# Three products of a feature group added in the same 128 PSUM columns, in place of two halves summed by VectorE

## The reference

```python
x = x + ffn0(cond0(x, itok, weights))        # the stage of this case
x = x + moe1(lora1(x, W, A, Bm, scalings, itok2))
# cond0: out[b, d, t] = sum_c x[b, c, t] * weights[itok[b]][c, d]     (64 x 64 per batch entry)
# ffn0:  gate_w, up_w, down_w = Catmull-Rom interpolations of control points, dense [2048 x 512]
#        inter = silu(h @ gate_w.T) * (h @ up_w.T);  out = inter @ down_w.T
```

## Time and profile before

| | |
|---|---|
| median of 3 runs | 1525.37 us |
| lowest and highest run | 1524.51, 1527.99 us |
| span of the profiled execution | 1560.4 us |
| busy in it: PE, PEld, DVE, ACT, POOL | 1373.9, 1236.1, 744.1, 441.3, 735.8 us |
| mean granted TensorE clock | 0.943 |

### The profile page before, as it was taken

How to read it: one execution, slowest core, us unless ns; L and a number is a source line. 1 busy time by engine, 2 the same in 40 slices (tenths; PEclk the granted TensorE clock), 3 DMA queues, 4 the chain that set the end, 5 groups by cost and what they waited for, 6 DMA issues and landing times. The chain is left out here.

```text
span 1560.4 us, 28551 instructions
## 1 busy us (share of the span) xinstructions
PE 1373.9 (88%) x8494; PEld 1236.1 (79%) x8495; DVE 744.1 (48%) x1603; ACT 441.3 (28%) x1025; POOL 735.8 (47%) x1199
## 2 busy tenths in 40 slices
PE   2131699999999999999999999947999999999996
PEld 1111588888888888888888889947999999989995
DVE  3298555555555555555554344432333333333332
ACT  3133333333333333333322322202222222222221
POOL 6608444454444444444452134433555555555554
PEclk9755799999999999999999899978999999999998
DMA  4034153222333333333332844312476476474443
GB/s 147 3 112 155 59 155 112 104 105 99 118 127 127 127 127 126 126 122 118 127 100 113 309 137 155 114 44 54 81 188 189 90 186 177 86 194 79 75 76 66
DMA packets 89920, 187.48 MB, mean 120 GB/s; under 512 B 15111, under 2 KB 40079, under 8 KB 85665
## 3 DMA queue, kind: packets, MB, share of 16 engines
q1 hardware_dynamic: 61778, 134.02, 25.0%
q0 software_dynamic: 22016, 43.35, 14.1%
q10 hardware_dynamic: 6096, 9.73, 1.8%
HBM read 110.97 MB, written 76.19 MB: 120 GB/s over the span
## 5 line engine op out<-in xcount | busy, mean ns | idle before, releaser
L948 POOL TENSOR_TENSOR in_lo<-inner,in_hi 128x256 fp32r<-128x256 f32 x256 | 187.2, 731 | 293.0 <-DVE in_hi L1144 293.0
L1023 PE MATMUL bank<-down_hi,in_hi 128*128 128x512 f32 x512 | 203.1, 397 | 0.0
L1024 PE MATMUL bank<-down_lo,in_hi 128*128 128x512 f32 x512 | 203.0, 396 | 0.0
L1025 PE MATMUL bank<-down_hi,in_lo 128*128 128x512 f32 x512 | 202.1, 395 | 0.0
L1654 PE MATMUL bank<-slots,zt_hi 128*128 x568 | 190.6, 336 | 4.6 <-DVE zt_lo L1743 3.0
L1576 POOL TENSOR_TENSOR idle<-small 128x1 f32<-128x1 f32 x284 | 93.6, 333 | 196.6 <-DMA out<-result,scatter_at 116.3
L1656 PE MATMUL bank<-slots,zt_lo 128*128 x568 | 183.7, 323 | 0.0
L1655 PE MATMUL bank<-slots,zt_hi 128*128 x568 | 183.0, 322 | 0.0
L972 PE MATMUL bank<-f_hi,gu_hi 92*128 92x256 f32 x512 | 161.7, 316 | 1.3 <-POOL f_lo L940 1.3
L1153 DVE TENSOR_TENSOR inner<-silu_all,bank 128x256 f32<-128x256 f32 x256 | 106.4, 416 | 83.9 <-ACT silu_all L1086 81.7
L973 PE MATMUL bank<-f_lo,gu_hi 92*128 92x256 f32 x512 | 144.2, 282 | 0.0
(11 more groups left out here) (218 smaller groups left out, 3283.7 us busy)
## 6 DMA issues: line engine op xcount, KB each, us to landing
gate_up_dram<-split_gu SPq DMA_DIRECT2D x16, 1408.0 KB, 4.9
slots<-gate_up_dram SPq DMA_DIRECT2D x16, 1408.0 KB
x_both<-in_x SPq DMA_DIRECT2D x32, 512.0 KB
expert_down_dram<-split_down SPq DMA_DIRECT2D x16, 768.0 KB, 7.2
slots<-expert_down_dram SPq DMA_DIRECT2D x16, 768.0 KB
out<-x_both SPq DMA_DIRECT2D x16, 512.0 KB, 3.2
x<-out SPq DMA_DIRECT2D x8, 1024.0 KB, 5.8
raw_down<-in_down_proj SPq DMA_DIRECT2D x16, 352.0 KB, 7.4
```

The source lines that it names most:

```text
L948: nc.gpsimd.tensor_tensor(in_lo[:, c % RING, :], inner[c % INNER][:, :], in_hi[:, c % RING, :].bitcast(F32), ALU.subtract).then_inc(in_don ...
L1023: nc.tensor.matmul(psum[bank][:, :], in_hi[:, c % RING, rows], down_hi[:, c, :], start=(c == 0), stop=False)
L1024: nc.tensor.matmul(psum[bank][:, :], in_hi[:, c % RING, rows], down_lo[:, c, :], start=False, stop=False)
L1025: ins = nc.tensor.matmul(psum[bank][:, :], in_lo[:, c % RING, rows], down_hi[:, c, :], start=False, stop=(c == IC - 1))
```

## The change

The three products of a half all go to the same 128 columns of the bank, so that the bank holds the finished sum and a tile's group takes 256 columns rather than 512. ScalarE copies from the bank to `f_hi`, VectorE subtracts from the bank to `f_lo` and raises `drained`, and `chunk` waits for that. `f_sum`, `f_done` and GpSimd's `features` are gone.

```diff
-        f_sum = [sb(f"f_sum{b}", [NF, TILE]) for b in range(2)]
...
-                def features(t, g):
-
-                    pool.wait_ge(f_high, GROUPS * t + g + 1)
-                    nc.gpsimd.tensor_tensor(f_lo[:, g, :], f_sum[g % 2][:, :], f_hi[:, g, :].bitcast(F32), ALU.subtract).then_inc(f_done, 1)
...
                     for s in range(SUB):
-                        at, both = psum[bank][0:NF, s * 2 * P:(s + 1) * 2 * P], pair[:, s, :, :].rearrange("p l n -> p (l n)")
-                        nc.tensor.matmul(at, feat_hi[:, s, g, :], both, start=True, stop=False)
-                        ins = nc.tensor.matmul(at[:, 0:P], feat_lo[:, s, g, :], pair_hi[:, s, :], start=False, stop=True)
+                        at = psum[bank][0:NF, s * P:(s + 1) * P]
+                        nc.tensor.matmul(at, feat_hi[:, s, g, :], pair_hi[:, s, :], start=True, stop=False)
+                        nc.tensor.matmul(at, feat_hi[:, s, g, :], pair_lo[:, s, :], start=False, stop=False)
+                        ins = nc.tensor.matmul(at, feat_lo[:, s, g, :], pair_hi[:, s, :], start=False, stop=True)
                     ins.then_inc(filled[bank], 1)
...
-                        pe.wait_ge(f_done, GROUPS * t + g + 1)
+                        pe.wait_ge(drained[feat_bank(t, g)], use_feat(t, g) + 2)
...
-                    act.wait_ge(drained[feat_bank(t, g)], use_feat(t, g) + 2)
-                    nc.scalar.activation(f_hi[:, g, :], f_sum[g % 2][:, :], ACT.Copy).then_inc(f_high, 1)
+                    bank = feat_bank(t, g)
+                    act.wait_ge(filled[bank], use_feat(t, g) + 1)
+                    nc.scalar.activation(f_hi[:, g, :], psum[bank][0:NF, 0:TILE], ACT.Copy).then_inc(f_high, 1)
...
-                    dve.wait_ge(filled[bank], use_feat(t, g) + 1)
-                    if not (first_tile(t) and g < 2):
-
-                        dve.wait_ge(f_done, GROUPS * t + g - 1)
-                    nc.vector.tensor_reduce(f_sum[g % 2][:, :].rearrange("p (s n) -> p s n", s=SUB),
-                                            view(psum[bank][0:NF, :], 0, [[2 * P, SUB], [1, P], [P, 2]]), AX.X, ALU.add).then_inc(drained[bank], 1)
+                    dve.wait_ge(f_high, GROUPS * t + g + 1)
+                    nc.vector.tensor_tensor(f_lo[:, g, :], psum[bank][0:NF, 0:TILE], f_hi[:, g, :].bitcast(F32),
+                                            ALU.subtract).then_inc(drained[bank], 1)
```

More of the change, by code:

```diff
@@ L763, in first_ffn @@
         cond_loaded, pair_high, pair_done = sem("cond_loaded"), sem("pair_high"), sem("pair_done")
-        mom_high, raw_high, f_high, f_done = (sem(n) for n in ("mom_high", "raw_high", "f_high", "f_done"))
+        mom_high, raw_high, f_high = (sem(n) for n in ("mom_high", "raw_high", "f_high"))
         raw_loaded, split_high = sem("raw_loaded"), sem("split_high")
@@ L935, in gather_cond, with body @@
                                                      bass.IndirectOffsetOnAxis(ap=cond_now[:, s:s + 1], axis=0)).then_inc(cond_loaded, 16)
-                def features(t, g):
-                    pool.wait_ge(f_high, GROUPS * t + g + 1)
-                    nc.gpsimd.tensor_tensor(f_lo[:, g, :], f_sum[g % 2][:, :], f_hi[:, g, :].bitcast(F32), ALU.subtract).then_inc(f_done, 1)
-                def body(t, gather, has_next):
+                def body(t, gather):
                     for c in range(IC):
-                        if first_tile(t) and c < FIRST_FEATS:
-                            features(t, GU_BANKS + c)
                         pool.wait_ge(in_high, IC * t + c + 1)
@@ L953, in body @@
                             gather_cond(t + 2)
-                        if has_next and c in FEAT_AT:
-                            features(t + 1, FEAT_AT[c])
                 gather_cond(0)
@@ L959, in _ @@
                 gather_cond(1)
-                for g in range(GU_BANKS):
-                    features(0, g)
-                body(0, True, True)
+                body(0, True)
                 with pool.Fori(1, NT - 1) as t:
-                    body(t, True, True)
-                body(NT - 1, False, False)
+                    body(t, True)
+                body(NT - 1, False)
                 pool.wait_ge(cond_loaded, 16 * SUB * (NT + 1))
```

## The result

| | before | changed |
|---|---|---|
| median, us | 1524.97 (4 runs, 1524.51 to 1527.99) | 1533.39 (4 runs, 1532.74 to 1535.08) |
| ratio | | 1.0055, 95% interval 1.0039 to 1.0071 |

The change makes the kernel slower by 8.4 us, 0.55%. The forecast was slower, 1530.2 within 1523.5 to 1535.5. In a second comparison the changed kernel stood at 1.0070 (1.0055 to 1.0085), 1536.59 against 1524.63.

A forecast was written before the change was run, and what follows sets the result against it. The prediction took TensorE to bound the feed-forward stage behind its first 37 us. Feature groups +11.3 us and the start -6.5 gave +4.8, carried over from the median 1525.37 to 1530.2 us, range 1523.5 to 1535.5.

The forecast's parts named there:

- Bound and cover: First feed-forward layer: TensorE bounds it behind the first 37 us and covers the other engines' work; no new wait, 0.
- A group on TensorE: Feature group: 316 ns becomes 5 x 82 = 410, 94 more; 120 groups outside tile 0 give +11.3 us.
- last slot: Slot of a feature group's last matmul: the load behind it belongs to the next line, before and after alike.
- The start: Tile 0: earlier f_lo brings the first down matmul 4.75 us earlier; with the clock staying full, -6.5 us together.
- with TensorE filled up to 175.1 ... I expect it to stay full: Tile 0: clock stays full, idle under half a microsecond at a time; 3.6 us of later half clock take 1.8.
- Rival 1: Tile 0: the clock falls again, start gives only -1.7 us; +9.6 us, 1535.0; chance 0.2.
- the rounds: Tile 0: three rounds of a group and a chunk, 2.14 us each before, estimated at 1.5 us after.
- The sum: Whole kernel: +11.3 - 6.5 = +4.8 us, carried over unscaled to 1530.2 us.
- Rivals 2 and 3: Feature groups: repeated feat_hi load free, 1524.7, chance 0.12; loads hide behind narrow matmuls, 1516.4, chance 0.06.
- Rival 4: Start gives back less, as unprofiled runs may lack the slump; between the forecast and 1536; chance 0.12.

The follow-up runs named there:

- wide kernel: Changed kernel with TensorE's feature matmuls of before (256 and 128 columns) and VectorE subtracting, then adding, in two steps; ratio to before 0.9991.
- before's second profile: The kernel before, unchanged, profiled once more beside the changed kernel; span 1524.5 us.
- the transposes ahead: Changed kernel plus twenty identity transposes into an idle bank in tile 0, before the wait for the condition pair; ratios to before 1.0068 and 1.0062.
- short loads: Changed kernel with 64 of 92 feature columns as weights in the feature matmuls, chunks keeping 92 rows; ratio to before 0.9965.

## Why the prediction was right, and where its sum was off

**Bound and cover: right.** TensorE is busy without a gap behind 200 us in the changed kernel too, and nothing waits for f_lo or the feature bank. The wide kernel shows that the other engines' part is worth nothing in steady state.

**A group on TensorE: right in kind, 9 ns low.** The slot was forecast at 82 ns and its starts are 0.08 apart; the runs with 64 and 128 columns of weights fix the cause. Per group the period gives 0.82/8 = 103 ns, not 94: +12.3 us, not +11.3. The surplus is in the last slot, which the prediction took to be the same before and after. That holds where a chunk follows (0.17 to L973 in the earlier trace rows, 0.17 to L960 after): averaged over the groups between 200 and 800 us, such a group, counted up to the second matmul behind it, costs 87 ns more than before. Where transposes follow, as behind three groups in four, it costs 108 to 113 more: read without rounding, the first two transposes are 0.11 apart in the kernel before and 0.13 in the changed one, as if their load began some 0.02 later. With loads of 128 columns it is 0.13 too, and with loads of 64 it is 0.12 to 0.13, so it is not the length of the load ahead of it; its cause stays open.

**The start: the mechanism right, its size wrong.** This is the mis-sized term: -6.5 us was forecast, and from the first transposes to the third tile's the two profiles give -1.1 and -1.6 (59.8 and 59.2 against 60.05 us of before's second profile, less the 0.82 of the one tile's groups in between; against its first, 59.84, 0.2 less). The step that failed is "with TensorE filled up to 175.1 ... I expect it to stay full": it looked only at idle time behind chunk 0, which the change takes away, and not at the idle time ahead of the features, which it leaves. The clock fell in that idle time or 0.4 us behind it in the two profiles, though in before's two it outlasted the same wait. Rival 1 had priced a fall (-1.7) rightly, but put it in the rounds. That the rest of the working was sound is shown where the clock stayed full. With the transposes ahead, the changed kernel's sixth group starts 3.6 us behind its first (forecast 3.6), the rounds take 1.63 us (forecast 1.5) and the start 8.2 (forecast 8.0); with short loads the rounds take 1.49 and the start 7.1. The stage was then 6.7 and 7.0 us above that of before's second profile, where 4.8 had been forecast: 12.3 less 5.6 and 5.3 at the start.

**The sum.** Forecast 11.3 - 6.5 = +4.8; the profiles' stages say 12.3 - 1.6 = +10.7 and, in the first, +11.2; the medians +8.4 and +12.0 us. So the direction and the larger term came out as reasoned, and that the time lies in the range is in part luck: by the stages it would stand at the range's upper edge (+10.1) or past it, and why the medians of the first comparison say less was not found. Rivals 2 and 3 (the repeated load free, the loads hidden) fall with the rows of one group: L989 has the weights of L988 once more, and from it to L990 it is 0.08, not 0.06. Rival 4 (runs without a profile have no slump at the start) stays open, as no such run shows its start.

**The slot of 81 ns.** The figure of about 81 ns that the Trainium skill, "TensorE: Matmul & The Clock Gate" (section "Back-to-back issue gap"), gives for a matmul over 128 columns in a stream of load and matmul pairs agrees with the 0.08 us measured here with loads of 92 columns. With the same 128 columns streamed, the slot is 0.06 with 64 columns of weights and 0.11 with 128, so from 92 columns up it is the load that sets it.

## What to carry to other kernels

Read the distance from start to start, not the recorded length, and compare each matmul's columns with those of the load behind it: a matmul that streams 128 columns before a load of 92 costs 82 ns instead of 59, so splitting a wide matmul costs time although no column is added. Where the clock is at stake, count the idle stretches that the change leaves, not only those that it removes, and read more than one profile before the clock of one is taken for the rule. And look first for whether a relieved engine is under the bound one: 35 us less on VectorE and 94 less on GpSimd brought nothing but the start.

## What the runs showed of the hardware that had not been expected

- Changing between matmuls of 64 rows and of 128 rows costs: at the change from 64 to 128 some 0.09 us more pass behind the matmul over 256 columns and 0.10 behind the next one over 512, and about the same on the way back. The kernel with 64-row chunks lost 6.1 us a tile (47.79 against 41.71), 0.38 for each chunk. With 92 rows no such loss is seen.
- The granted clock can fall or not about the same idle wait. The wait was 2.4 and 1.8 us in the changed kernel, where the clock fell in it or 0.4 us behind it, 2.54 in before's second profile and 2.65 in the kernel with 64-column loads and 92 rows, where it didn't. In eight profiles the fall came where TensorE had run for 1.4 us or less at full clock ahead of the wait, and not where it had run for 1.5 or more. What decides was not tested.
- The first two transposes behind narrow matmuls alone are some 0.02 us further apart (0.13) than behind a wide and a narrow one (0.11).
